# Two scatter-add targets, 59 tiles and a mask shift among the tiles, in a two-layer graph and expert kernel

## Chip, core and metric

The kernel runs on one core of a Trainium2 chip. Times are microseconds (us) of device time of that core, from one execution of the whole program; the median of a few executions is given, with the lowest and highest. The profiled execution is a further one, and its own time stands beside its span. Engines are called TensorE (PE; its weight loads PEld), VectorE (DVE), ScalarE (ACT), GpSimd (POOL) and SyncE (SP); "SPq" and "ACTq" in a row are DMA issues of those engines.

## The reference

There are 3327 nodes with 256 features each and a 3327 x 3327 adjacency. Two layers follow each other; each is an attention over the neighbours and then a mixture of 8 experts of which every node uses 2.

```
x = x + gelu(graph_attention_0(layernorm(x), adj))        # 1 head
x = x + experts_0(layernorm(x))                            # 8 experts, hidden 512, top 2
x = x + graph_attention_1(layernorm(x), adj)               # 4 heads, plus projection of x
x = x + experts_1(layernorm(x))                            # 8 experts, hidden 1024, top 2

experts(x): logits = x @ gate + b; top 2 of softmax -> weights w
            out[n] = sum over the 2 experts e of n: w[n,e] * (gelu(x[n] @ W1[e] + b1[e]) @ W2[e] + b2[e])
```

## The kernel before

The nodes are padded to 26 tiles of 128 rows (T = 26, NP = 3328). All matmuls of the experts are fp32. The program is a row of blocks; in a block every engine has its own stream, and a block ends when all engines have ended theirs. In order: the first attention, the first experts' routing, the first experts' tiles, a small block that reads x back, the second attention (a block for its values and reaches, a block for the attention itself), the second experts' routing and their tiles.

**Routing.** Each node has two slots, one for each of its experts. Slots of one expert are packed into tiles of 128 slots; `expert_of[g]` is the expert of tile g, `slot_row[:, g]` the DRAM row of each slot and `slot_w[:, g]` its weight. Slots that hold no node point at spare rows behind the 3328. The kernel before runs RUN_TILES = 2T + 8 = 60 tiles and keeps SLOT_TILES = 62 columns.

**A tile g** (slot s = g % 2 of every ring of two) goes through these steps, which each engine does in the order of g:

- SP (`tiles_sync`, L1594): when the hidden products of tile g are done, load W1 of tile g+2 into slot s (512 KB in the first experts, 1 MB in the second).
- POOL (`tiles_gpsimd`): L1611 gathers the 128 rows of tile g+4 from `xs` into one of four buffers `rx`; L1626 scatter-adds the weighted result `ry[s]` into the rows of `total` in DRAM (`xd` in the first experts, `out` in the second). The two slots of a node can lie in any two tiles, and an accumulating transfer reads, adds and writes, so the kernel lets only one scatter be in flight.
- PE (`tiles_tensor`): `hidden` of tile g+1 (L1637), the transposes `turn_x` of tile g+2 (L1644), the second product y of tile g (L1674), in this order.
- ACT (`tiles_scalar`): copies the transposed x (L1684, or L1688 in the second experts) and takes the Gelu of the hidden rows (L1703).
- DVE (`tiles_vector`): adds b2 (L1718) into `ysum`, multiplies by the slot's weight (L1721) into `ry[s]`.

The wait that orders the scatters, in POOL's stream:

```
pool.wait_ge(self.ry_ready[g % 2], g // 2 + 2)
if g > 0:
    pool.wait_ge(self.added, 16 * g)                 # scatter g-1 has landed
    pool.sem_inc(self.ry_free[(g - 1) % 2], 1)       # DVE may write ry of g+1
pool.indirect_dma_start(total[...], ... self.ry[g % 2], compute_op=ALU.add).then_inc(self.added, 16)
```

DVE waits on `ry_free[s]` before it adds b2 for the next tile of slot s. TensorE waits on `ry_ready[s]` before it writes the y bank of slot s again.

**Between the layers.** `xd` holds x plus the experts' sum. A block of its own reads it back into X with one DMA on SP (L1726, 3.4 MB), while DVE shifts the whole adjacency mask left by 3 bits as 32-bit words (L1904, 21632 words a partition, in place). Then semaphores are cleared, all engines meet, and the next block starts: bn_stats over the 26 tiles of X (L1735) for the layer norm, six loads of weights on SP (L340 to L350), and the values' products, for which TensorE waits for all six.

Of the kernel before, what the change touches and what calls it, by code (L numbers as in the profile page):

```python
# [28 lines left out]
ALU = mybir.AluOpType  # L29
# [24 lines left out]
RUN_TILES = 2 * T + 8  # L54
SLOT_TILES = RUN_TILES + 2
# [34 lines left out]
def program(nc, x_in, adjT, w0T, w0, r0, w1, w1T, uv1, proj_wT, bias1, proj_b1,  # L90
            gate0, gate_b0, m0w1, m0b1, m0w2, m0b2, gate1, gate_b1, ln_g1, ln_b1, m1w1, m1b1, m1w2, m1b2,
            qd, xd, xs, out):
    ctx = ExitStack()
    with ctx:
# [75 lines left out]
        spare_clean = sem("spare_clean")  # L170
        id_zero = sem("id_zero")
# [51 lines left out]
        class Attention:  # L223
            def __init__(self, L, tag):
# [54 lines left out]
                self.w_loaded = sem(tag + "w_loaded")  # L279
                self.stat = sem(tag + "stat")  # L280
# [54 lines left out]

            def values_sync(self, sp):
# [15 lines left out]
            def values_vector(self, v):  # L352
                L, H = self.L, self.L.H
                v.memset(self.ones_row[:, :], 1.0).then_inc(self.reach_best, 1)
                layer_norm_stats(v, self)
# [840 lines left out]
        class Experts:  # L1196
            def __init__(self, hidden, tag, weights_at, scratch_at, second_norm):
# [91 lines left out]
                def ring(n, size):  # L1289
# [33 lines left out]
                self.x_back = sem(tag + "x_back")  # L1323
# [10 lines left out]
                self.added = sem(tag + "added")  # L1334
                self.ry_free = [sem(f"{tag}ry_free{s}") for s in range(2)]
                start_at_one.extend(self.tp_ready + self.xt_ready + self.xn_ready + self.tx_ready + self.xgt_ready
                                    + self.h_ready + self.ht_ready + self.y_ready + self.ry_ready + self.ry_free
# [251 lines left out]
            def tiles_sync(self, sp, w1m, b1m, b2m):  # L1589
# [11 lines left out]
                with sp.Fori(0, RUN_TILES // 2) as i:  # L1601
                    for s in range(2):
                        sp.wait_ge(self.h_ready[s], i + 2)
                        load_w1(2 * i + s + 2, s)
                for s in range(2):
                    sp.wait_ge(self.w1_loaded[s], 16 * (RUN_TILES // 2 + 1))

            def tiles_gpsimd(self, pool, total):
# [7 lines left out]
                for g in range(RUN_TILES):  # L1616
                    if g + 4 < SLOT_TILES:
# [8 lines left out]
                    pool.indirect_dma_start(total[:, :],  # L1626
                                            bass.IndirectOffsetOnAxis(ap=slot_row[:, g:g + 1], axis=0),
                                            self.ry[g % 2], None, compute_op=ALU.add).then_inc(self.added, 16)
                pool.wait_ge(self.added, 16 * RUN_TILES)

            def tiles_tensor(self, pe):
# [24 lines left out]
                with pe.Fori(0, RUN_TILES // 4) as j:  # L1656
                    for q in range(4):
                        i, s = 2 * j + q // 2, q % 2
                        o = 1 - s
                        g = 4 * j + q  # L1660

                        pe.wait_ge(self.w1_loaded[o], 16 * (i + s + 1))
# [3 lines left out]

# [381 lines left out]
```

## Time and profile before

| | |
|---|---|
| median of 3 runs | 2111.42 us (2108.45 to 2119.23) |
| profiled execution, its own time | 2120.95 us |
| its span, first to last instruction | 2119.3 us |
| PE busy (share of span) | 1706.8 us (81%) |
| DVE, ACT, POOL busy | 973.2, 1045.1, 499.4 us (46%, 49%, 24%) |
| granted TensorE clock, mean | 0.916 |
| DMA moved | 188.84 MB, mean 89 GB/s |

Busy time is the time an engine spent in instructions; what is between is idle, and the profile names what ended each idle time. Over the span the first experts' tiles lie at 556 to 905 us, the block between the layers at 906 to 919, the second attention at 919 to about 1620 and the second experts' tiles at 1662 to the end. "Landing" of a DMA is the time from its issue on the engine to its last byte. A granted clock of 1.00 is TensorE at its full 2.4 GHz, 0.50 is 1.2 GHz.

### The profile page before, as it was taken

The page shows a single profiled execution, that of the slowest core. Times are in us where ns is not written, and L with a number is a line of the kernel's source. Part 1 is how long each engine was busy: PE and PEld are TensorE (multiplying, and loading weights), DVE is VectorE, ACT ScalarE, POOL GpSimd, SP SyncE. Part 2 cuts the span into 40 slices and gives each one's busy share as a digit, 9 for nine tenths or more (in the row PEclk, how much of TensorE's full clock was granted, in tenths as well). Part 3 has the DMA queues.
Part 4 walks back from the last instruction along what each step waited for, and adds up shares of the span by engine and source line. Part 5 has one row for each costly group of instructions (what it writes and reads, how often), then busy time and mean ns, then how long its engine had stood idle before and what let it go on. Part 6 is the DMA issues. An engine that isn't in the chain of part 4 may idle for free. (4 is left out here: it accounts for less than half of the span.)

```text
span 2119.3 us, 44107 instructions
## 1 busy us (share of the span) xinstructions
PE 1706.8 (81%) x13058; PEld 1560.1 (74%) x13059; DVE 973.2 (46%) x2091; ACT 1045.1 (49%) x2152; POOL 499.4 (24%) x565
## 2 busy tenths in 40 slices
PE   4659999955687778646489797897965799999998
PEld 3448888845676667535488797897965799999997
DVE  4548888875411111166576666765675311111111
ACT  1634444444144343302478787787854255445444
POOL 1100000000144444400750712600000133333332
PEclk9969999985799999968699999999985899999999
DMA  9930000023365565520000000000016466666665
GB/s 145 108 46 8 15 7 15 13 77 131 95 151 144 140 146 138 122 87 12 6 15 9 16 12 12 16 8 16 15 54 234 141 182 187 174 180 190 173 178 146
DMA packets 78483, 188.84 MB, mean 89 GB/s; under 512 B 9658, under 2 KB 49878, under 8 KB 69206
## 3 DMA queue, kind: packets, MB, share of 16 engines
q1 hardware_dynamic: 50630, 144.50, 20.7%
q0 software_dynamic: 26976, 43.07, 13.8%
q8 instruction: 29, 0.48, 0.1%
q10 hardware_dynamic: 816, 0.53, 0.1%
q14 instruction: 32, 0.26, 0.0%
HBM read 191.47 MB, written 29.83 MB: 104 GB/s over the span
## 5 line engine op out<-in xcount | busy, mean ns | idle before, releaser
L1185 PE MATMUL bank<-arena 128*128 128x195 bf16 x5408 | 478.6, 249 | 103.1 <-DVE arena L1086 44.4
L1185 PEld LDWEIGHTS bank<-arena 128*128 128x128 fp8e4 x5408 | 466.8, 98 | 114.8 <-issue 113.2
L996 ACT ACTIVATE arena<-arena,m_row 128x512 fp8e5<-128x512 f32 (+1 forms) x728 | 431.8, 677 | 131.1 <-DVE arena L1086 119.1
L1674 PE MATMUL bank<-arena,X 128*128 x1440 | 343.2, 389 | 29.4 <-issue 25.4
L1718 DVE TENSOR_TENSOR arena<-bank,X 128x256 f32<-128x256 f32 x120 | 50.9, 425 | 682.4 <-PE bank L1674 460.2
L1637 PEld LDWEIGHTS bank<-X,arena 128*128 128x128 f32 x2928 | 353.1, 195 | 6.8
L1637 PE MATMUL bank<-X,arena 128*128 128x128 f32 x2928 | 352.6, 278 | 0.0
L1674 PEld LDWEIGHTS bank<-arena,X 128*128 128x128 f32 x1440 | 268.1, 193 | 74.0 <-issue 41.6
L856 PE MATMUL bank<-arena 128*128 (+1 forms) x1352 | 299.6, 383 | 14.7 <-DVE arena L799 14.7
L856 PEld LDWEIGHTS bank<-arena 128*128 128x128 f32 x1352 | 257.0, 191 | 56.4 <-issue 20.6
L777 ACT ACTIVATE bank<-arena,s_all 128x384 f32<-128x384 f32 (+1 forms) x234 | 133.9, 573 | 183.0 <-DVE arena L791 175.8
L1084 DVE SCALAR_TENSOR_TENSOR arena<-arena 128x512 uint32<-128x512 uint32 (+2 forms) x196 | 131.9, 673 | 173.3 <-ACT arena L996 106.7
L1703 ACT ACTIVATE X<-bank,arena 128x128 f32<-128x128 f32 x720 | 199.3, 379 | 18.3 <-issue 17.6
L1611 POOL DMA_INDIRECT arena<-xs,slot_row x124 | 122.3, 986 | 203.3 <-POOLq L1847 164.7
L791 DVE SCALAR_TENSOR_TENSOR arena<-arena,d_all,bank 128x384 f32<-128x384 f32 (+1 forms) x234 | 139.7, 597 | 63.5 <-PE bank L856 47.2
L1688 ACT ACTIVATE X<-bank,arena 128x128 f32<-128x128 f32 x124 | 50.1, 454 | 237.9 <-PE bank L1644 237.9
L1626 POOL DMA_INDIRECT out<-X,slot_row x60 | 95.5, 1592 | 275.3 <-DVE X L1721 240.6
L1626 POOL DMA_INDIRECT xd<-X,slot_row x60 | 98.0, 1633 | 167.7 <-issue 140.6
L1585 POOL IOTA arena<- 128x128 f32 x2 | 0.5, 240 | 574.4 <-POOLq L1820 363.5
L1086 DVE SCALAR_TENSOR_TENSOR arena<-arena 128x512 uint32<-128x512 uint32 (+2 forms) x196 | 132.6, 677 | 0.0
L799 DVE TENSOR_TENSOR arena<-arena 128x384 f32<-128x384 f32 (+1 forms) x234 | 124.7, 536 | 0.0
L1684 ACT COPY X<-bank 128x256 f32<-128x256 f32 x62 | 23.1, 373 | 198.4 <-PE bank L1644 198.4
(204 smaller groups left out, 1406.0 us busy)
## 6 DMA issues: line engine op xcount, KB each, us to landing
arena<-m1w SPq DMA_DIRECT2D x70, 1024.0 KB, 5.8
arena<-m0w SPq DMA_DIRECT2D x70, 512.0 KB, 3.6
arena<-adjT POOLq DMA_DIRECT2D x26, 416.0 KB, 12.9
xs<-X SPq DMA_DIRECT2D x4, 1664.0 KB, 6.9
arena<-qd SPq DMA_DIRECT2D x25, 256.0 KB, 3.3
X<-x_in SPq DMA_DIRECT2D x2, 1664.0 KB, 11.5
xd<-X SPq DMA_DIRECT2D x13, 256.0 KB, 2.2
X<-xd SPq DMA_DIRECT2D x1, 3328.0 KB, 12.0
```

The source lines that it names most:

```text
L777: a.activation(self.exp_bank[s][:, 0:nt * P], self.rows[r][:, 0:nt * P], ACT.Exp, bias=s_all[:, at(c, 1)]).then_inc(self.exp_ready[s], 1)
L791: v.scalar_tensor_tensor(out=self.prob[q][:, 0:w], in0=self.rows[r][:, W:W + w], scalar=d_all[:, at(c, 1)], in1=self.exp_bank[s][:, 0:w], ...
L799: v.tensor_tensor(self.prob[q][:, 0:w], self.prob[q][:, 0:w], mask[:, at(c * NP + b * W, w)], ALU.min).then_inc(self.prob_ready[q], 1)
L856: last = pe.matmul(bank[3 * r + n][:, 0:D + 1], self.prob[q][:, n * P:(n + 1) * P], V[:, at(c * VW, D + 1)], start=False, stop=False, skip ...
L996: last = a.activation(self.sign[slot].bitcast(F8W)[:, q * W:q * W + nt * P], self.row[r][:, 0:nt * P], ACT.Sigmoid, scale=STEEP, bias=self ...
L1084: v.scalar_tensor_tensor(out=pos, in0=sg, scalar=1, in1=m, op0=ALU.logical_shift_left, op1=ALU.bitwise_and).then_inc(self.pos_ready, 1)
L1086: v.scalar_tensor_tensor(out=neg, in0=sg, scalar=0x08080808, in1=m, op0=ALU.bitwise_xor, op1=ALU.bitwise_and).then_inc(self.neg_ready[slot ...
L1185: last = pe.matmul(bank[r * NT + n][:, kind * KW:(kind + 1) * KW], self.split[slot][kind].bitcast(F8)[:, q * W + n * P:q * W + (n + 1) * P ...
L1626: pool.indirect_dma_start(total[:, :], bass.IndirectOffsetOnAxis(ap=slot_row[:, g:g + 1], axis=0), self.ry[g % 2], None, compute_op=ALU.ad ...
L1637: last = pe.matmul(bank[2 * s + c // 4][:, c % 4 * P:(c % 4 + 1) * P], self.W1[s][:, k * HID + c * P:k * HID + (c + 1) * P], self.rxt[s][: ...
L1674: last = pe.matmul(bank[5 + s][:, 0:D], self.ht[s][:, c * P:(c + 1) * P], self.W2[:, at(e * (HC * D) + c * D, D)], start=(c == 0), stop=(c ...
L1703: last = a.activation(self.ht[s][:, c * P:(c + 1) * P], bank[2 * s + c // 4][:, c % 4 * P:(c % 4 + 1) * P], ACT.Gelu, bias=self.b1[:, at(e ...
```

## The change

1. RUN_TILES and SLOT_TILES become 2T + 7 = 59 (`2 * T + E - 1`). The loops no longer run `hidden`, `turn_x` and W1 loads for tiles beyond the last; the last one to three tiles stand behind the loops as straight code (both experts).
2. First experts: even tiles scatter-add into `xd`, odd ones into a new DRAM tensor `xe`. POOL no longer waits for the scatter before; DVE waits for the scatter of tile g-2 (`added[s]`) before it writes `ysum` and `ry[s]`. The second experts still have one target and keep POOL's wait; there too DVE waits on `added[s]` directly, and `ry_free` is gone.
3. `xe` is filled with zeros by one DMA of POOL (27 x 128 rows of 1 KB) in the block of the first attention.
4. The block between the layers is gone. The mask shift is cut into 26 slices of 832 words, one ahead of each pair of tiles 2 to 53 in DVE's tile loop of the first experts.
5. The second attention's first block loads `xd` into X in four parts on SP and `xe` into the arena in four parts on ACT; for each part DVE adds the two and runs bn_stats on its tiles. The six loads of weights move from SP's queue to ACT's, behind the four parts.

```diff
-RUN_TILES = 2 * T + 8
-SLOT_TILES = RUN_TILES + 2
+RUN_TILES = 2 * T + E - 1
+SLOT_TILES = RUN_TILES
...
+            def back_load(self, eng, which):
+                tiles = [T * c // self.BACK for c in range(self.BACK + 1)]
+                to, of = ((X, xd), (words(V_AT, T * D), xe))[which]
+                for c in range(self.BACK):
+                    a, b = tiles[c], tiles[c + 1]
+                    eng.dma_start(to[:, a * D:b * D].rearrange("p (t d) -> p t d", d=D),
+                                  of[a * P:b * P, :].rearrange("(t p) d -> p t d", p=P)).then_inc(self.x_back[c], 16)
+            def back_vector(self, v):
...
+                    v.wait_ge(self.x_back[c], 32)
+                    v.tensor_tensor(X[:, a * D:b * D], X[:, a * D:b * D], other[:, a * D:b * D], ALU.add
+                                    ).then_inc(self.x_whole, 1)
+                    v.wait_ge(self.x_whole, c + 1)
+                    for t in range(a, b):
+                        v.bn_stats(stats[:, at(t * 6, 6)], X[:, at(t * D, D)]).then_inc(self.stat, 1)
...
-                    if g > 0:
-                        pool.wait_ge(self.added, 16 * g)
-                        pool.sem_inc(self.ry_free[(g - 1) % 2], 1)
-                    pool.indirect_dma_start(total[:, :],
+                    if n_to == 1 and g > 0:
+                        pool.wait_ge(self.added[(g - 1) % 2], 16 * ((g - 1) // 2 + 1))
+                    pool.indirect_dma_start(totals[g % n_to][:, :],
...
-                        v.wait_ge(self.ry_free[s], i + 1)
+                        v.wait_ge(self.added[s], 16 * i)
...
+                slices = 26
+                size = MASK_WORDS // slices
+                for s in range(2):
+                    tile(0, s)
+                with v.Fori(1, slices + 1) as i:
+                    if not self.second_norm:
+                        m32 = words(MASK_AT, MASK_WORDS).bitcast(U32)[:, at((i - 1) * size, size)]
+                        v.tensor_scalar(m32, m32, 3, None, ALU.logical_shift_left)
+                    for s in range(2):
+                        tile(i, s)
...
+                pool.dma_start(xe.rearrange("(t p) d -> p t d", p=P),
+                               zeros[:, :].bitcast(F32).rearrange("p (o d) -> p o d", o=1).to_broadcast([P, T + 1, D])
+                               ).then_inc(xe_clean, 16)
...
-        with nc.Block() as block:
-            @block.sync
-            def _(sp):
-                X0.back_sync(sp)
-            @block.vector
-            def _(v):
-                m32 = words(MASK_AT, MASK_WORDS).bitcast(U32)
-                v.tensor_scalar(m32, m32, 3, None, ALU.logical_shift_left)
...
             @block.sync
             def _(sp):
+                A1.back_load(sp, 0)
                 give_ones(sp, q1_ones)
-                A1.values_sync(sp)
                 A1.own_row_sync(sp)
...
             @block.scalar
             def _(a):
+                A1.back_load(a, 1)
+                A1.values_sync(a)
```

## Rows read from the trace of the kernel before

**Rows 1.** Busy time by stretch: bounds, length, PE, PEld, DVE, ACT, POOL with counts, clock, DMA share, GB/s

```profile
577.49:589.20 11.71, 11.70 (x80) 10.63 (x79) 2.38 (x6) 7.67 (x21) 5.92 (x5) 1.00 0.79 187
620.00:820.00 200.00, 153.02 (x945) 130.09 (x944) 28.61 (x74) 78.66 (x202) 96.13 (x73) 1.00 0.59 143
1700.00:2090.00 390.00, 390.00 (x2691) 367.70 (x2691) 41.87 (x108) 195.84 (x567) 139.08 (x108) 1.00 0.64 181
```

**Rows 2.** Waits, 620 to 880 us: who waited for whom, total, times, longest

```profile
DVE arena L1718 <- POOLq L1625: 192.8, 42, 6.1
...
PE bank L1644 <- DMA arena<-xs,slot_row: 34.9, 40, 2.4
```

**Rows 3.** Timeline, 700 to 722 us: start, length, engine, instruction, idle before it

```profile
702.91 1.71 POOL L1626 DMA_INDIRECT xd<-X,slot_row  x1 [2.59 <-issue]
...
704.92 0.99 POOL L1611 DMA_INDIRECT arena<-xs,slot_row  x1 [0.30 <-issue]
...
707.97 0.42 DVE L1718 TENSOR_TENSOR arena<-bank,X 128x256 f32<-128x256 f32 x1 [4.81 <-POOLq L1625]
...
708.20 0.44 PE L1644 MATMUL bank<-ident,arena 128*128 128x128 f32 x2 [0.96 <-DMA arena<-xs,slot_row]
...
708.56 1.59 POOL L1626 DMA_INDIRECT xd<-X,slot_row  x1 [2.65 <-issue]
```

**Rows 4.** Timeline, 574 to 590 us, the first tiles

```profile
574.67 0.35 DVE L1721 TENSOR_SCALAR X<-arena,slot_w 128x256 f32<-128x256 f32 x1
575.31 1.64 POOL L1626 DMA_INDIRECT xd<-X,slot_row  x1 [13.93 <-DVE X L1721]
...
575.98 1.89 PE L1674 MATMUL bank<-arena,X 128*128 x8
...
581.68 1.95 PE L1637 MATMUL bank<-X,arena 128*128 128x128 f32 x16
...
589.41 1.95 PE L1637 MATMUL bank<-X,arena 128*128 128x128 f32 x16
```

**Rows 5.** DMA queues, 575 to 903 us: packets, MB, share of 16 engines

```profile
q1 hardware_dynamic: 8352, 30.41, 30.2%
q0 software_dynamic: 11376, 15.34, 27.7%
```

**Rows 6.** DMA issues, 577 to 590 us: count, size, median us to landing

```profile
arena<-m0w SPq DMA_DIRECT2D x4, 512.0 KB, 4.2
```

**Rows 7.** Line L1626: ns minimum/median/maximum, and landing in 575 to 903 us

```profile
L1626 POOL DMA_INDIRECT xd<-X,slot_row x60: 1546/1588/1711, 575.3 to 899.2; - x60
...
DMA to landing us min/median/max: 3.7/4.6/5.9
```

**Rows 8.** Timeline, 880 to 985 us: last scatter, read-back block, statistics

```profile
899.16 1.55 POOL L1626 DMA_INDIRECT xd<-X,slot_row  x1 [2.97 <-DMA xd<-X,slot_row]
905.97 0.40 SPq L1726 DMA_DIRECT2D X<-xd  x1
906.00 11.43 DVE L1904 TENSOR_SCALAR arena<-arena 128x21632 uint32<-128x21632 uint32 x1 [11.05 <-PEq L1868]
...
919.50 8.59 DVE L1735 BATCH_NORM_STATS2 stats<-X  x26
...
928.12 0.20 DVE L1740 TENSOR_TENSOR mv<-stats 128x26 f32<-128x26 f32 x1
```

**Rows 9.** The page's DMA issues: count, size, median us to landing

```profile
X<-xd SPq DMA_DIRECT2D x1, 3328.0 KB, 12.0
```

**Rows 10.** Timeline, 2095 to 2120 us, the last tiles of the second experts

```profile
2099.85 3.62 PE L1674 MATMUL bank<-arena,X 128*128 x16
...
2107.10 3.62 PE L1674 MATMUL bank<-arena,X 128*128 x16
...
2112.62 1.55 POOL L1626 DMA_INDIRECT out<-X,slot_row  x1 [3.96 <-DVE X L1721]
```

**Rows 11.** Timeline, 520 to 600 us, one step of the first routing

```profile
531.72 0.99 DVE L1485 TENSOR_TENSOR X<-tile_no,arena 128x806 f32<-128x806 f32 x1
```

More of the change, by code:

```diff
@@ L91, in program @@
             gate0, gate_b0, m0w1, m0b1, m0w2, m0b2, gate1, gate_b1, ln_g1, ln_b1, m1w1, m1b1, m1w2, m1b2,
-            qd, xd, xs, out):
+            qd, xd, xe, xs, out):
     ctx = ExitStack()
@@ L279, in __init__ @@
                 self.w_loaded = sem(tag + "w_loaded")
+                self.x_back = [sem(f"{tag}x_back{c}") for c in range(4 * (H > 1))]
+                self.x_whole = sem(tag + "x_whole")
                 self.stat = sem(tag + "stat")
@@ L1655, in tiles_tensor, with tile @@
                 pe.wait_ge(self.w2_loaded, 16 * 8)
[L1656 to L1660, printed above, removed]
+                def tile(j, q):
+                    i, s = 2 * j + q // 2, q % 2
+                    o = 1 - s
+                    g = 4 * j + q
+                    left = 4 if not isinstance(j, int) else RUN_TILES - 1 - g
+                    if left >= 1:
                         pe.wait_ge(self.w1_loaded[o], 16 * (i + s + 1))
@@ L1725, in back_sync, with tile @@
[L1725 to L1735 removed]
+                def tile(i, s):
+                    g = 2 * i + s
+                    e = v.value_load(expert_of[0:1, at(g, 1)], min_val=0, max_val=E - 1)
+                    v.wait_ge(self.y_ready[s], i + 2)
+                    if not isinstance(i, int) or i > 0:
+                        v.wait_ge(self.added[s], 16 * i)
+                    v.tensor_tensor(self.ysum[s], bank[5 + s][:, 0:D], self.b2[:, at(e * D, D)], ALU.add
+                                    ).then_inc(self.ysum_ready, 1)
+                    v.wait_ge(self.ysum_ready, g + 1)
+                    v.tensor_scalar(self.ry[s], self.ysum[s], slot_w[:, at(g, 1)], None, ALU.mult
+                                    ).then_inc(self.ry_ready[s], 1)
@@ new lines, in tiles_vector @@
+                slices = 26
+                size = MASK_WORDS // slices
+                for s in range(2):
+                    tile(0, s)
[3 more added lines that the diff above has]
+                        v.tensor_scalar(m32, m32, 3, None, ALU.logical_shift_left)
+                    for s in range(2):
+                        tile(i, s)
+                with v.Fori(slices + 1, RUN_TILES // 2) as i:
+                    for s in range(2):
+                        tile(i, s)
@@ L1736, in layer_norm_stats @@
+                tile(RUN_TILES // 2, 0)
+        def layer_norm_stats(v, sems, nth=1, done=False):
+            if not done:
+                with v.Fori(0, 2) as half:
+                    for q in range(PAIRS):
+                        t = half * PAIRS + q
+                        v.bn_stats(stats[:, at(t * 6, 6)], X[:, at(t * D, D)]).then_inc(sems.stat, 1)
             v.wait_ge(sems.stat, T * nth)
```

112 lines of the change are left out of this document (59 added, 53 removed).

## The prediction

> **What bounds the kernel now.** I read the table of busy time by stretch first. In the first experts' tiles the engines leave room: over 620 to 820 us TensorE is busy 153 of 200 us at full clock, GpSimd 96, and the DMA engines 59% [rows 1]. So no engine is the bound, and the waits have to say what is. Over 620 to 880 us (48 tiles) VectorE waits 192.8 us for GpSimd's semaphore instruction at L1625, the one that follows the wait for the scatter before, and TensorE waits 34.9 us for gathers at L1644 [rows 2].
>
> The timeline shows the ring. A scatter starts at 702.91 and the next at 708.56, 5.65 us later; GpSimd works 1.71 us on the first, issues a gather for 0.99, then sits idle for 2.65 until the scatter has landed [rows 3]. VectorE starts its add at 707.97, when the semaphore is given. The gather of four tiles ahead stands behind the scatter in GpSimd's stream, so it comes late too, and TensorE's transpose at 708.20 has waited 0.96 for it [rows 3]. The period of a tile is the scatter's way through: 323.85 us between the first scatter (575.31) and the last (899.16) over 59 intervals [rows 4, 8], 5.49 us each.
>
> How fast could it be? The first tiles tell, before the backlog of scatters reached TensorE. There the hidden products of two tiles apart start at 581.68 and 589.41: 7.73 us, 3.87 a tile [rows 4]. In that stretch TensorE is busy for all of its 11.7 us, and the DMA share is 79% [rows 1]. The second experts are different: TensorE is busy for all 390 us from 1700 to 2090 [rows 1], and a tile takes 7.25 [rows 10]. They are bound by it.
>
> **The change part by part.** The sum is made against the profiled execution: span 2119.3 us, own time 2120.95, which is 9.5 above the median of 2111.42. I take the difference in us from the one to the other unchanged.
>
> *Two targets.* The wait for scatter g-1 goes. What is late next? Four candidates for the period of a tile:
> - TensorE: 3.87 us [rows 4].
> - GpSimd: scatter 1.59, gap 0.30, gather 0.99 [rows 3, 7], and 0.29 from the end of VectorE's multiplication (574.67 + 0.35) to the scatter [rows 4]: 3.17 us. If each scatter is as long as the longest, 1.71, 3.29.
> - The ring of one slot, now over two tiles: add and multiplication 0.9, start 0.3, landing 4.6 (longest 5.9) [rows 3, 4, 7], some 0.2 for the semaphore: 6.0 to 7.3 us for two tiles, so 3.0 to 3.65.
> - W1: a load can be issued when hidden g ends and is needed when hidden g+2 starts, 2 x 3.87 - 1.95 = 5.8 us later. In the free stretch loads landed in 4.2 us [rows 6], which leaves 1.6 for issue and queueing.
>
> All four are under 3.87 but the first, and none by much. The DMA engines give the reason for a little more: they were taken 57.9% of a 5.49 us period [rows 5], 3.18 us of work a tile, or 82% of 3.87. The free stretch ran at 79% without a wait of TensorE, though with fewer scatters. I take 3.95 us, near the row of the free stretch; the bounds are 3.8 (TensorE no slower than its best pair) and 4.4 (W1 landing 1.7 us later than it did, at 5.9, which sets (1.95 + 0.9 + 5.9) / 2; the 0.9 of issue lag is my estimate from the 1.6 that are free).
>
> The y product of tile 1 starts at 575.98 [rows 4] in both. Tile 58 follows 57 periods later; at 3.95 that is 801.1, less 1.0 because the last tile has no hidden product ahead of it and waits only for its Gelu (1.95 saved, some 1 for the wait, an estimate): 800.1. Product 2.0, VectorE and start 1.3, landing 3.9 (between the least and the median [rows 7], since no W1 load is beside it): 807.2. The last scatter of before landed at 899.16 + 3.9 = 903.1. Gain 95.9.
>
> *The shift.* 11.43 us in one instruction beside the 12.0 us load [rows 8, 9] cost nothing before, and 26 slices of 0.44 us cost nothing now, since VectorE is busy 28.6 of 200 us [rows 1]. At worst each slice delays VectorE's tile by 0.44, within the slot ring's slack. There is another way in which it can cost. GpSimd's scatter takes 1.71 instead of 1.59 when VectorE's 0.35 us multiplication runs at its start [rows 3, 7], so 0.12 is what an overlap cost here.
>
> The Trainium skill ("SBUF — State Buffer", Who interferes with whom) says more: a tensor_scalar in a 2-port mode and GpSimd lock each other out for the whole instruction. By that, 0.44 every second tile and the whole 0.35 each tile would be added to GpSimd's 3.17, an estimate of 3.74 a tile; the sum, which goes by TensorE's 3.87, would stay. The trace has the 0.12 only, and nowhere a slice beside a scatter.
>
> *Between the layers.* Before: from landing (903.1) to the layer norm's statistics (928.12) 25.0 us: 2.9 to the next block's DMA at 905.97, 13.5 of load and block change, 8.6 of bn_stats [rows 8]. After: the same 2.9, and 1.2 of the 1.5 that lie between the load's landing (905.97 + 12.0) and the first bn_stats, for clearing semaphores and the meeting of all engines; then 6.8 MB instead of 3.4. The load of before took 12.0 us for 3.4 MB [rows 9]; with 2.3 of it taken as start (an estimate) it ran at 350 GB/s. I take the two queues as sharing that rate, for one queue already feeds all 16 engines [rows 5]: 19.5 + 2.3 + 0.5 for issues = 22.3. Behind the last quarter come an add of 1792 columns, 1.9 (VectorE did 806 in 0.99, of which a part is fixed [rows 11]; 256 in 0.42 [rows 3]), and 7 bn_stats at 0.33, 2.3. Together 30.7: 5.7 lost. Bounds: if the queues add their rates, 12.0 + 0.5 + 4.2 + 4.1 = 20.8, a gain of 4.2; if they take turns at the full 24.0, a loss of 7.8. The six weight loads are queued behind `xe` on ScalarE's queue, and everything that TensorE does next waits for them; 1 MB more (by the tensors' shapes) is 3 us behind 22.3, landing about when the statistics are ready, so hidden. The sqrt on ScalarE stands behind ten issues of 0.40 [rows 8], 4 of the 26 us there are.
>
> *59 tiles and straight ends.* In the second experts y of tile 58 starts at 2099.85, of 59 at 2107.10, and takes 3.62; the other 3.6 of the period of 7.25 are the hidden products [rows 10]. Now y of tile 58 is the last and has none ahead of it: it ends 7.25 + 3.6 = 10.9 earlier. Its scatter may meet the one before still landing, so I give back 0.4: gain 10.5. Bounds: 7.3 (if a wait for Gelu takes the place of the hidden product) and 10.9.
>
> *Smaller tables.* Twelve operations of 806 columns at 0.99 [rows 11] become 767: 0.04 each, 0.5 a layer, with the matmuls 0.6; gain 1.2.
>
> *Zeroing `xe`.* 3.4 MB in the first attention, whose window has hundreds of us with DMA nearly idle; its first row loads could be 2 us late. Taken as 0.5, bounds 0 and 3.
>
> Sum: 95.9 - 5.7 + 10.5 + 1.2 - 0.5 = 101.4. The profiled execution's 2120.95 would be 2019.5, and the median 2111.4 - 101.4 = 2010. Each 0.1 us of period is 5.7 us.
>
> **Rivals.**
> - *Transfers become the bound.* With 82% of the DMA engines taken, W1 or the scatters land later and the period is 4.15 to 4.7. For it: landings grew from 3.7 to 5.9 already [rows 7], and 4.2 for W1 in the dense stretch. Against: no wait for W1 at 79% [rows 1]. At 4.4 the gain is 101.4 - 57 x 0.45 = 76: 2036.
> - *GpSimd becomes the bound.* 3.17 is the least; if the slices and VectorE's multiplications shut it out for their whole length and each start takes 0.9 rather than 0.3, it takes 3.17 + 0.22 + 0.35 + 0.6 = 4.34 a tile: 22 less, 2032. The rule quoted above is what would bring it about; the row's 0.12 speaks against.
> - *The order moves only a little.* Something else keeps the tile near 5.2, for instance gathers that still wait for their place in GpSimd's stream: gain 101.4 - 57 x 1.25 = 30, 2081. Against: with the scatter's wait gone GpSimd has 0.7 us to spare in each tile.
> - *Slower than before.* Two accumulating scatters in flight slow each other, so that the slot ring sets the period. It is (1.4 + landing) / 2; the gains are used up at 3.95 + 101.4 / 57 = 5.73 us, that is from a landing of 10.1 us, where the longest of 60 was 5.9 [rows 7]. At 11 the period is 6.2 and the time 2138.
>
> **How the numbers follow.** Forecast (period 3.8 to 4.15, so 2001 to 2021, and 1997 with part of the reload's bound) 0.65; transfers 0.15; GpSimd 0.08; little moved 0.08; slower 0.02; 0.02 for others near no change. The likeliest is 2010. The range of 8 in 10 takes in the transfers' and GpSimd's cases: 1997 to 2038. A change under 0.5% (10.6 us) is about what a measurement of this kernel can't tell from none; faster by more than that 0.95, within 0.03, slower 0.02.
>
> **What would show it.** Hidden products of the first experts 3.85 to 4.0 us apart, TensorE busy over 95% between 580 and 800 us at clock 1.00, VectorE's wait for POOLq gone and replaced by a wait for the y product; GpSimd waiting for VectorE ahead of each scatter. Rows of TensorE waiting for `arena<-m0w` would show the first rival; scatters above 1.8 us the second. The statistics would end some 30 us after the last scatter's landing, and the last scatter of the program would start 6.7 us before the end, as it does now. The forecast fails if the free stretch was free only because few scatters were in flight.

## The result, and the profile of the changed kernel

| | before | after |
|---|---|---|
| median | 2112.49 us (2108.45 to 2119.23, 4 runs) | 2016.78 us (2016.21 to 2018.66, 4 runs) |
| profiled execution, its own time | 2120.95 us | 2017.3 us |
| its span | 2119.3 us | 2015.4 us |
| PE busy (share of span) | 1706.8 us (81%) | 1665.5 us (83%) |

The ratio of the times is 0.9528, with a 95% interval of 0.9506 to 0.9551: the changed kernel is faster by 4.7%. The forecast was 2010, with a range of 1997 to 2038. Between the profiled executions 103.65 us are gained, between the medians 95.7.

The busy time by stretch, after (columns as in [rows 1]):

```profile
600.00:760.00 160.00, 159.81 (x1077) 146.29 (x1076) 44.45 (x104) 90.24 (x230) 112.08 (x84) 1.00 0.79 203
...
805.00:850.00 45.00, 16.51 (x67) 13.14 (x68) 27.25 (x70) 4.12 (x9) 0.00 (x0) 0.61 0.57 176
...
1640.00:2000.00 360.00, 360.00 (x2491) 339.58 (x2490) 38.90 (x100) 179.26 (x523) 126.13 (x97) 1.00 0.63 177
```

In the first experts' tiles TensorE is now busy 159.8 of 160 us, where it was 153 of 200 [rows 1]. The DMA share is 79%, the same as in the free stretch of before. The waits of that stage, 580 to 790 us:

```profile
DVE arena L1764 <- PE bank L1705: 137.0, 52, 3.2
...
POOL xd L1655 <- DVE X L1767: 26.1, 27, 1.3
POOL xe L1655 <- DVE X L1767: 22.7, 28, 1.9
...
DVE arena L1764 <- DMA xe<-X,slot_row: 5.8, 2, 3.0
PEld bank L1667 <- DMA arena<-m0w: 0.5, 1, 0.5
```

VectorE's wait for GpSimd's semaphore [rows 2] is gone; it waits for TensorE's y product (L1705). GpSimd waits for VectorE's result (L1767) ahead of each scatter (L1655). Only twice did VectorE wait for a scatter two tiles back, and once TensorE for a load of W1. The same in time, 701 to 708 us:

```profile
701.47 1.95 PE L1667 MATMUL bank<-X,arena 128*128 128x128 f32 x16
...
702.34 0.35 DVE L1767 TENSOR_SCALAR X<-arena,slot_w 128x256 f32<-128x256 f32 x1
702.76 0.59 DVE L1777 TENSOR_SCALAR arena<-arena  x1
702.97 1.84 POOL L1655 DMA_INDIRECT xe<-X,slot_row  x1 [0.75 <-DVE X L1767]
...
705.12 0.99 POOL L1641 DMA_INDIRECT arena<-xs,slot_row  x1 [0.30 <-issue]
...
705.45 1.95 PE L1667 MATMUL bank<-X,arena 128*128 128x128 f32 x16
...
707.05 1.59 POOL L1655 DMA_INDIRECT xd<-X,slot_row  x1 [0.94 <-DVE X L1767]
```

The scatters are 4.08 us apart here, and GpSimd is ready 0.75 and 0.94 us before their data are. Hidden products start at 701.47, 705.45 and, behind what is shown, 709.18: 7.71 us for two tiles. The scatters and the shift by their lines (lengths in ns, minimum/median/maximum):

```profile
L1655 POOL DMA_INDIRECT xd<-X,slot_row x30: 1547/1591/1632, 575.5 to 797.0; - x30
L1655 POOL DMA_INDIRECT xe<-X,slot_row x29: 1547/1841/1867, 579.2 to 795.2; - x29
...
L1777 DVE TENSOR_SCALAR arena<-arena x26: 587/594/595, 578.8 to 772.3; - x26
```

The DMA queues, 575 to 800 us:

```profile
q1 hardware_dynamic: 7920, 28.84, 45.4%
q0 software_dynamic: 11051, 14.79, 31.3%
```

The boundary between the layers, 797 to 834 us:

```profile
797.02 1.55 POOL L1655 DMA_INDIRECT xd<-X,slot_row  x1 [0.30 <-issue]
804.68 6.24 SPq L348 DMA_DIRECT2D X<-xd  x4
804.69 7.73 ACTq L348 DMA_DIRECT2D arena<-xe  x4
812.44 5.10 ACTq L368 DMA_DIRECT2D arena<-w  x1
...
823.42 0.45 ACTq L378 DMA_DIRECT2D arena<-proj_b  x1
...
827.16 2.02 DVE L358 TENSOR_TENSOR X<-X,arena 128x1792 f32<-128x1792 f32 x1 [0.66 <-DMA arena<-xe]
829.22 2.38 DVE L362 BATCH_NORM_STATS2 stats<-X 128x6 f32<-128x256 f32 x7
830.36 1.85 PE L447 MATMUL bank<-arena 128*128 128x8 f32 x8 [34.80 <-DMA arena<-proj_b]
...
831.66 0.18 DVE L1796 TENSOR_TENSOR mv<-stats 128x26 f32<-128x26 f32 x1
```

The last of the eight loads let VectorE go at 827.16, 22.5 us after the first was issued. And the end of the program, where [rows 10] showed it before:

```profile
1999.50 7.07 PE L1705 MATMUL bank<-arena,X 128*128 x32
...
2004.46 1.55 POOL L1655 DMA_INDIRECT out<-X,slot_row  x1 [5.38 <-DVE X L1767]
...
2008.89 1.55 POOL L1655 DMA_INDIRECT out<-X,slot_row  x1 [2.88 <-DMA out<-X,slot_row]
```

The y products of the last two tiles follow each other without a hidden product between them.

Stage by stage, the profiled execution before against that after (in us, bounds by the first and last scatters and the first `mv<-stats`, the start of the layer norm's statistics):

| | before | after | gain | forecast |
|---|---|---|---|---|
| start to first scatter | 575.31 | 575.48 | -0.2 | +0.1 (tables, zeroing) |
| first to last scatter, first experts | 323.85 | 221.54 | 102.3 | 95.9 |
| last scatter to statistics | 28.96 | 34.64 | -5.7 | -5.7 |
| statistics to first scatter, second experts | 756.58 | 759.97 | -3.4 | +0.6 (tables) |
| first to last scatter, second experts | 427.92 | 417.26 | 10.7 | 10.5 |
| last scatter to end | 6.68 | 6.51 | 0.2 | 0 |
| sum | | | 103.9 | 101.4 |

### The profile page after: what moved, and what is told of

Read it like the earlier page. It is cut to its first block and busy times, and to the rows that moved or that the text cites. A ratio compares the mean times of both kernels' runs of the same rounds, so it can differ in the third digit from the quotient of the medians.

```text
span 2015.4 us, 43515 instructions
## 1 busy us (share of the span) xinstructions
PE 1665.5 (83%) x12926; PEld 1536.0 (76%) x12927; DVE 980.1 (49%) x2116; ACT 1033.3 (51%) x2127; POOL 497.2 (25%) x558
## 5 line engine op out<-in xcount | busy, mean ns | idle before, releaser
L1667 PEld LDWEIGHTS bank<-X,arena 128*128 128x128 f32 x2832 | 337.8, 194 | 6.5 <-DMA arena<-m0w 0.5
L1667 PE MATMUL bank<-X,arena 128*128 128x128 f32 x2832 | 338.2, 277 | 0.1
L1705 PE MATMUL bank<-arena,X 128*128 x1416 | 329.2, 383 | 4.6 <-ACT X L1740 4.4
L884 PE MATMUL bank<-arena 128*128 (+1 forms) x1352 | 299.6, 383 | 15.5 <-DVE arena L827 15.5
L1705 PEld LDWEIGHTS bank<-arena,X 128*128 128x128 f32 x1416 | 260.8, 191 | 42.0 <-issue 11.0
L1740 ACT ACTIVATE X<-bank,arena 128x128 f32<-128x128 f32 x708 | 195.9, 379 | 25.4 <-issue 19.9
L1641 POOL DMA_INDIRECT arena<-xs,slot_row x118 | 116.6, 988 | 201.2 <-issue 117.5
L1725 ACT ACTIVATE X<-bank,arena 128x128 f32<-128x128 f32 x118 | 47.7, 454 | 223.7 <-PE bank L1674 223.7
L1655 POOL DMA_INDIRECT out<-X,slot_row x59 | 93.9, 1592 | 270.2 <-DVE X L1767 267.4
L1048 POOL TENSOR_TENSOR arena<-arena,neg_sj 128x130 f32 x46 | 27.2, 592 | 275.3 <-PEq L1221 143.9
```

The source lines that it names most:

```text
L884: last = pe.matmul(bank[3 * r + n][:, 0:D + 1], self.prob[q][:, n * P:(n + 1) * P], V[:, at(c * VW, D + 1)], start=False, stop=False, skip ...
L1641: pool.indirect_dma_start(self.rx[g % 4], None, xs[:, :], bass.IndirectOffsetOnAxis(ap=slot_row[:, g:g + 1], axis=0)).then_inc(self.rx_loa ...
L1667: last = pe.matmul(bank[2 * s + c // 4][:, c % 4 * P:(c % 4 + 1) * P], self.W1[s][:, k * HID + c * P:k * HID + (c + 1) * P], self.rxt[s][: ...
L1705: last = pe.matmul(bank[5 + s][:, 0:D], self.ht[s][:, c * P:(c + 1) * P], self.W2[:, at(e * (HC * D) + c * D, D)], start=(c == 0), stop=(c ...
L1740: last = a.activation(self.ht[s][:, c * P:(c + 1) * P], bank[2 * s + c // 4][:, c % 4 * P:(c % 4 + 1) * P], ACT.Gelu, bias=self.b1[:, at(e ...
```

## The experiments

Each kernel is the changed one with the edit shown, run beside the kernel before; ratios are to the kernel before. Kernels with a single execution have no interval.

**The second target taken back.** Even and odd tiles add into `xd` again, with GpSimd's wait; everything else of the change stays.

```diff
-        experts_blocks(X0, [xd, xe], a1_ones, gate0, ...
+        experts_blocks(X0, [xd], a1_ones, gate0, ...
```

> The changed kernel with one edit undone: in the first experts all tiles scatter-add into xd again, and GpSimd waits for the scatter before, as in the second experts. xe is still zeroed, loaded and added. Theory (the wait for the one scatter in flight set the period): the scatters of the first experts are 5.3 to 5.5 us apart again, VectorE or TensorE wait behind that ring, and the time is 2016.8 + 57 x 1.55 + some 4 us of tail = 2104 to 2112 us. Rival (the gain came mostly from fewer tiles, straight ends and the moved shift): the period stays under 4.5 us and the time under 2055 us.

Measured 2106.95 us, ratio 0.9946 (0.9919 to 0.9972). Eight of its nine executions lie between 2093.28 and 2109.83; the ninth took 3023.88, at a mean granted clock of 0.554 where the others had 0.912 to 0.918. What lowered it is not known, and without it the median would be 2106.43. The waits of 620 to 860 us:

```profile
DVE arena L1764 <- DMA xd<-X,slot_row: 185.9, 44, 5.2
...
POOL xd L1655 <- DMA xd<-X,slot_row: 107.7, 43, 3.4
```

The ring is back: 312.46 us from the first scatter to the last over 58 intervals, 5.39 each. The kernel before took 5.49 in one profile and 5.08 in another (below), so this lies between them. So it is the second target that brings the stage's gain, down to 3.82 an interval; of the shift, the straight ends and VectorE's direct wait on `added`, together, no part of it is seen.

**Only the shorter tiles.** One target, the old block between the layers, the shift in one piece, no `xe`; 59 tiles, straight ends and the smaller tables stay.

```diff
-        experts_blocks(X0, [xd, xe], a1_ones, gate0, ...
+        experts_blocks(X0, [xd], a1_ones, gate0, ...
+        with nc.Block() as block:      # sync: one load of xd into X; vector: the whole shift
...
-                A1.back_load(sp, 0)
+                A1.values_sync(sp)
```

> Only part 1 of the change: 59 tiles, smaller tables and straight ends in both experts, with one target, the read-back block with the whole mask shift, and no xe. Theory: 10.5 us from the end of the second experts, one tile of about 5.4 us in the first, 1.2 us from the tables, so 17 us under the kernel before: about 2095 us. The difference to the run with one target is the price of reading and adding two buffers, 5 to 6 us by the trace. Rival (straight code behind the loops costs instruction loading of several us at each end): 2100 us or more, with gaps of over 2 us at the ends of the loops.

Measured 2097.53 us (2087.84 to 2102.82), ratio 0.9912 (0.9877 to 0.9948). Its scatters are 5.34 us apart, and the statistics come 28.56 us after the last one, as before (28.96). It lies 9.4 us under the kernel above. Between the last scatter of the first experts and the first of the second there are 788.5 us here and 795.6 there, 5.6 of it up to the statistics: the new way of reading back costs something there too, and it has no use with one target.

**The kernel before, once more,** to see how much of its time varies and where.

> The kernel before once more, for a second profile. Its runs spread over 12 us, those of the changed kernel over 2.5 us, and the profiled execution of before lies 8.5 us above its median. Theory (the ring of scatters makes the time of the first experts' tiles depend on DMA landings and on stalls of TensorE that lower its clock): the stretch from the first to the last scatter differs from the 323.9 us of the first profile by several us, and the rest of the program by less than 2. Rival (the spread lies elsewhere, in the mask load or the attentions): the stretch is the same within 1 us.

Measured 2096.7 us. Its scatters:

```profile
L1626 POOL DMA_INDIRECT xd<-X,slot_row x60: 1547/1588/1708, 575.3 to 875.2; - x60
```

From first to last 299.84 us, 5.08 a tile, against 323.85 in the profiled execution of before. The spans differ by 24.2 us (2095.1 and 2119.3), this stage by 24.0; the rest takes 1795.2 and 1795.5. So these two executions of the kernel before differ in the ring of scatters and nowhere else. The landings make the difference: added up over the stage's 60 scatters they come to 275.8 us in the first profile (4.6 in the middle) and 251.9 here (3.9), and the rest of a period, from a landing to the next scatter, is 0.88 on average in both. Why they land sooner here is not known. This execution is also faster than all 17 others of the kernel before in its set (2104.34 to 2122.57). In eight executions of the changed kernel and its variants with two targets and whole tiles (the two of the changed kernel, and those with thirteen parts, three shifts, the shift taken out, no load of `xe` and the two early reloads) the stage took 221.4 to 222.7 us.

**The changed kernel, once more,** beside three of its variants.

> The changed kernel once more, on the chip of the next two runs, for a comparison without the spread of the kernel before. Both theories: 2016 to 2018 us, its runs within 3 us, and 221.5 us from the first to the last scatter of the first experts.

Measured 2019.32 us (2017.44 to 2020.13), ratio 0.9534 (0.951 to 0.9558). Scatters 222.0 us from first to last, then 34.40 to the statistics. The same program's median was 2016.78 in the first set of runs: 2.5 us are between two sets, and less than that is not told apart across sets. The two profiles differ by 2.8 us in their spans, and by 3.1 in the stretch from the statistics to the second experts' first scatter (759.97 and 763.06): what varies in the changed kernel lies there and not in the first experts' tiles.

**No load of `xe`.** The odd tiles' sums are left out of the second layer's input.

```diff
-                    v.wait_ge(self.x_back[c], 32)
-                    v.tensor_tensor(X[:, a * D:b * D], X[:, a * D:b * D], other[:, a * D:b * D], ALU.add ...
+                    v.wait_ge(self.x_back[c], 16)
...
-                A1.back_load(a, 1)
```

> The changed kernel without the load of xe and without the adds: the second layer works on xd alone, so the odd tiles' sums are left out. It prices the second buffer in the read-back. Theory (the two loads share one rate of some 350 GB/s, so the second costs its bytes): from the first load's issue to the layer norm's statistics 27.0 falls to 15.5 us, that is 12 us of load, 2.4 of bn_stats of the last quarter and 1; 11 us faster, about 2006 us. Rival (two queues add their rates): the loads of one buffer take as long as those of two, only the adds of 1.9 us go, 2015 us.

Measured 2010.62 us (2007.56 to 2011.92), ratio 0.9494 (0.9465 to 0.9523), 8.7 us under the changed kernel of the same set. The boundary:

```profile
805.21 5.16 SPq L348 DMA_DIRECT2D X<-xd  x4
805.21 0.48 ACTq L365 DMA_DIRECT2D arena<-w  x1
...
821.93 2.39 DVE L359 BATCH_NORM_STATS2 stats<-X 128x6 f32<-128x256 f32 x7 [0.42 <-DMA X<-xd]
...
824.37 0.18 DVE L1793 TENSOR_TENSOR mv<-stats 128x26 f32<-128x26 f32 x1
```

From issue to statistics 19.2 us, against 27.0 with both loads (804.68 to 831.66). I had worked out 15.5, with the 12.0 of a load alone [rows 9]. But half of `xd` now shared its rate with the weights on the other queue, and it landed 16.7 us after its issue. So the second load costs 7.8 us, and the second queue adds no rate that is seen: 3.4 MB on one took 12.0 us [rows 9], 6.8 MB on two 22.5.

**Thirteen parts instead of four** in the reload.

```diff
-            BACK = 4
+            BACK = 13
```

> The changed kernel with the read-back in 13 parts of two tiles each instead of 4 parts. Behind the last landing stand an add of 512 columns and 2 bn_stats, about 1.3 us, instead of 4.4 us. Theory (the last part's VectorE work is on the path): 2 to 3 us faster, 2014 to 2015 us. Rival (ScalarE's queue takes its issues more slowly than the loads move, the third and later parts of xe are late, and the weights land after the statistics): same or up to 5 us slower.

Measured 2014.01 us (2010.07 to 2016.1), ratio 0.9526 (0.95 to 0.9553). The boundary:

```profile
802.99 10.93 SPq L348 DMA_DIRECT2D X<-xd  x13
802.99 11.86 ACTq L348 DMA_DIRECT2D arena<-xe  x13
...
826.31 0.68 DVE L358 TENSOR_TENSOR X<-X,arena 128x512 f32<-128x512 f32 x1
827.02 0.75 DVE L362 BATCH_NORM_STATS2 stats<-X 128x6 f32<-128x256 f32 x2
```

The statistics come 32.45 us after the last scatter, 2.2 less than with four parts: the add and the bn_stats behind the last part fell from 4.4 to 1.4 us, and not all of it came out at the end, since VectorE now has 0.69 + 0.75 a part for 13 parts and runs nearly without a pause from the third on. The whole time's interval overlaps that of the changed kernel, and the medians, 2.8 us apart, are of two sets, so the 2.2 us are shown by the trace alone.

**The shift three times as long.** Three shifts by one bit in place of one by three.

```diff
-                        v.tensor_scalar(m32, m32, 3, None, ALU.logical_shift_left)
+                        for _n in range(3):
+                            v.tensor_scalar(m32, m32, 1, None, ALU.logical_shift_left).then_inc(self.shifted, 1)
+                            v.wait_ge(self.shifted, 3 * i - 2 + _n)
```

> The changed kernel with each slice of the mask shift done as three shifts by 1 instead of one by 3: three VectorE instructions of 0.59 us in the same mode and place, 1.8 us and their waits for each pair of tiles. Theory (VectorE and GpSimd have room in a pair of 7.7 us, and an overlap delays a scatter by some tenths of a us): the period stays 3.86 us and the time 2015 to 2019. Rival (the Trainium skill's rule, SBUF - State Buffer, Who interferes with whom: such an instruction and GpSimd lock each other out for its whole length, so 1.2 us more go onto GpSimd's 6.7 us of a pair, which makes 7.9 and more than TensorE's 7.7): scatters beside the slices take 2.5 us and more, the period is 3.95 to 4.2 and the time 2022 to 2036.

Measured 2017.07 us (2012.92 to 2017.95), ratio 0.9552 (0.9498 to 0.9606). One pair of tiles:

```profile
701.93 1.95 DVE L1779 TENSOR_SCALAR arena<-arena  x3
702.14 1.84 POOL L1656 DMA_INDIRECT xe<-X,slot_row  x1 [0.76 <-DVE X L1768]
```

The shifts of the whole stage by their line (ns, minimum/median/maximum):

```profile
L1779 DVE TENSOR_SCALAR arena<-arena x78: 585/594/704, 578.0 to 772.7; - x78
```

VectorE shifts from 701.93 to 703.88, and the scatter that starts at 702.14 takes 1.84 us, as beside one shift. The scatters' stage took 221.52 us (221.54 with one). These are three instructions of 0.59 us, though, and not one of three times the length. The scatter starts 0.21 us into the first, as it does with a single shift, and is lengthened by 0.25 where 0.38 of that shift was left. So the run shows that VectorE has room for 1.4 us more in a pair of tiles (1.95 for 0.59); it does not show what one long shift would do to a scatter.

The Trainium skill ("SBUF — State Buffer", Who interferes with whom) has the second of the two engines shut out until the first one's instruction is over, where VectorE's is a `tensor_scalar` in a 2-port mode. For the start of the scatter the trace agrees roughly (0.25 of the 0.38 left), for the rest of it not: the scatter is running when the second shift comes, 0.41 us after its start, and that shift takes its 0.59 us, while the third, at 1.04, takes 0.70.

**The shift out of the tiles,** in one piece at the start of the second layer.

```diff
-                    if not self.second_norm:
-                        m32 = words(MASK_AT, MASK_WORDS).bitcast(U32)[:, at((i - 1) * size, size)]
-                        v.tensor_scalar(m32, m32, 3, None, ALU.logical_shift_left)
...
+                v.tensor_scalar(m32, m32, 3, None, ALU.logical_shift_left)
                 A1.back_vector(v)
```

> The changed kernel with the mask shift taken out of the tile loop and done in one instruction of 11.4 us ahead of the adds of the read-back. Theory (the slices cost nothing among the tiles; here 8 us of the shift lie in the wait for the first quarter, and VectorE's chain of 11.4 + 17 us is 1 to 2 us longer than the 27 us of the reload): the tile stretch is the same within 0.5 us, the scatters into xe take 1.59 us instead of 1.84, and the time is 1 to 3 us above the changed kernel's, 2018 to 2020. Rival (the slices hold up the tiles): the stretch from the first to the last scatter is several us shorter than 221.5 us.

Measured 2018.66 us (2015.46 to 2021.44), ratio 0.9562 (0.9508 to 0.9617). The scatters into `xe` are short again:

```profile
L1655 POOL DMA_INDIRECT xe<-X,slot_row x29: 1547/1587/1592, 575.8 to 792.8; - x29
```

And yet the stage took 222.64 us, not less. GpSimd's 0.25 us were paid out of its idle time ahead of the scatters. At the boundary 35.41 us instead of 34.64: there the 11 us shift hides behind the reload, nearly all of it.

**What comes next if TensorE has less to do.** Half of the first experts' hidden product is left out.

```diff
                     for c in range(HC):
-                        for k in range(KC):
+                        kk = KC if self.second_norm else 1
+                        for k in range(kk):
```

> The changed kernel with half of the first experts' hidden product left out (only the first 128 of the 256 features are multiplied), so that TensorE needs about 0.9 us less a tile, 2.97 us. It shows which bound stands next. Theory (GpSimd, with scatter 1.59 to 1.84, gather 0.99 and gaps): 3.4 us a tile, GpSimd without idle time beyond 0.3 us gaps and VectorE or TensorE waiting for it; time about 2016.8 - 57 x 0.45 = 1991. Rival 1 (DMA engines and W1): TensorE waits for the loads of W1, 3.3 to 3.7 us a tile. Rival 2 (landing of the scatter two tiles before): VectorE waits for DMA, 3.0 to 3.5 us a tile.

Measured 2013.81 us, in one execution. The scatters took 214.5 us, 3.70 a tile, though TensorE had 0.98 us less a tile. The whole time fell by less than these 7 us, since the stretch from the statistics to the second experts took 763.6 here, near the upper end of its spread. The waits of 580 to 785 us:

```profile
DVE arena L1765 <- DMA xe<-X,slot_row: 29.2, 13, 2.9
...
DVE arena L1765 <- DMA xd<-X,slot_row: 23.3, 10, 2.7
...
PEld bank L1675 <- DMA arena<-xs,slot_row: 13.2, 17, 1.4
```

The next bound is not GpSimd. VectorE waited 23 times for the scatter two tiles back, and TensorE for gathers. Landings took 5.1 and 5.3 us in the middle here, 6.1 at most, where one scatter in flight had 4.6 [rows 7].

**The same with an eighth of W1's bytes** from the third tile on (the hidden products then use old weights).

```diff
-                    sp.dma_start(self.W1[s], w1m[:, at(e * size, size)]).then_inc(self.w1_loaded[s], 16)
+                    part = size if (self.second_norm or isinstance(g, int) and g < 2) else size // 8
+                    sp.dma_start(self.W1[s][:, 0:part], w1m[:, at(e * size, part)]).then_inc(self.w1_loaded[s], 16)
```

> As the run with half of the first experts' hidden product left out, and from tile 2 on each load of W1 brings one eighth of its bytes, the rest of W1 staying that of the first two tiles. It takes most of the load off the DMA engines. If GpSimd is the next bound, the period stays at that of the run with full loads, within 0.05 us. If W1 or the DMA engines are, it falls to 3.2 us or lower.

Measured 1991.43 us, in one execution. 195.2 us of scatters, 3.37 a tile. The queues, 575 to 769 us:

```profile
q0 software_dynamic: 10812, 14.57, 46.8%
q1 hardware_dynamic: 7920, 3.61, 6.4%
```

With the hardware queue at a seventh, only one wait of VectorE for a scatter is left (1.7 us). Gathers landed in 2.8 us in the middle, where they took 3.8 with W1 loaded whole. So it was the W1 loads beside them that kept the transfers long enough to be waited for; the scatters' own landings are not in this profile. At 3.37 the period comes near GpSimd's 3.17 to 3.29, which the prediction had added up. GpSimd is still not the bound alone: ahead of the scatters into `xd` it waited 28 times for VectorE, 21.9 us in all. What sets the 3.37 stays open.

**The reload issued at the end of the tiles' block,** by SP and ScalarE themselves, in 13 parts, as soon as both `added` semaphores are complete.

```diff
+        def early_back(X_, eng, which):
+            for s in range(2):
+                eng.wait_ge(X_.added[s], 16 * (RUN_TILES // 2 + 1 - s))
+            A1.back_load(eng, which)
...
                     X_.tiles_sync(sp, w1m, b1m, b2m)
+                    if ln is None:
+                        early_back(X_, sp, 0)
```

> The changed kernel with the read-back in 13 parts and issued inside the block of the first experts' tiles, by SP and ScalarE as soon as the last scatters of both buffers have landed, so that the end of the block, the clearing of semaphores and the meeting of all engines run beside the loads. Theory: 2 us from the 13 parts and 3 to 4 us from the earlier issue, 2010 to 2012 us. Rival (issues of 13 parts on ScalarE hold up the block's end, or the engines meet later than the loads land): no more than the 2 us of the parts, 2014 to 2015 us.

Measured 2016.31 us (2015.41 to 2019.45), ratio 0.953 (0.9505 to 0.9554). The boundary:

```profile
794.55 1.55 POOL L1655 DMA_INDIRECT xd<-X,slot_row  x1 [0.31 <-issue]
798.41 10.56 ACTq L348 DMA_DIRECT2D arena<-xe  x13
...
810.89 0.69 DVE L358 TENSOR_TENSOR X<-X,arena 128x512 f32<-128x512 f32 x1 [16.76 <-PEq L1968]
```

The loads are issued 3.9 us after the last scatter instead of 7.7. But the block cannot end before ScalarE and SP have got rid of their 13 issues, 10.6 us, and VectorE's adds stand behind the block's end. The statistics come 34.43 us after the last scatter (34.40 in the changed kernel of the same set): nothing gained at that place. The median is 3.0 us lower and the executions overlap, so no gain of time is shown either.

**The same with the adds and the weights' loads in the tiles' block too.**

```diff
                     X_.tiles_vector(v)
+                    if ln is None:
+                        A1.back_vector(v)
...
+                        early_back(X_, a, 1)
+                        A1.values_sync(a)
```

> As the run with 13 parts issued inside the block of the first experts' tiles, and VectorE's adds and bn_stats and ScalarE's loads of weights stand in that block too, so that nothing of the read-back waits for the change of blocks. Theory (in the run before it the block's end held VectorE back for 10 us of issues): the loads start 4 us after the last scatter instead of 7.6, VectorE follows each part as it lands, and the statistics are ready some 30 us after the last scatter instead of 34.6: 4 us under the changed kernel, about 2013 to 2015 us. Rival (the change of blocks, now behind the reload, costs what it saved): 2016 to 2018 us.

Measured 2014.51 us (2012.35 to 2015.24), ratio 0.9528 (0.9501 to 0.9556). The boundary:

```profile
797.59 1.55 POOL L1655 DMA_INDIRECT xd<-X,slot_row  x1 [0.30 <-issue]
...
805.64 0.69 DVE L358 TENSOR_TENSOR X<-X,arena 128x512 f32<-128x512 f32 x1 [8.44 <-DMA X<-xd]
...
826.90 1.85 PE L447 MATMUL bank<-arena 128*128 128x8 f32 x8 [30.80 <-DMA arena<-proj_b]
...
828.86 0.17 DVE L387 COPY arena<-bank 128x16 f32<-128x16 f32 x1 [0.28 <-PE bank L447]
```

Statistics 29.3 us after the last scatter, 5.3 less; the copy behind the weights' product (L387) 31.3 after it instead of 36.4, since now that product comes last. Its executions lie all under those of the changed kernel run again (2017.44 to 2020.13), by 4.8 us in the medians. The two were not run in one set, and the changed kernel's medians have differed by 2.5 between sets; so the 5 us at the boundary are shown by the trace, and their full size in the time is not shown. Nor is this version shown to be faster than the one with thirteen parts alone, whose median is 2014.01 and whose ratio is 0.9526.

## Why the prediction was right, point by point

- **The bound.** Right. The scatters' ring was the bound and TensorE took its place: 99.9% busy, with the period of its free stretch. 56 periods of y products, from 576.05 to 791.94, give 3.855 us a tile. I had read 3.87 there [rows 4] and taken 3.95, for fear of the DMA load. The DMA engines' load came somewhat below what I had worked out (3.18 us a tile, 82% of the period): 76.7% over the stage with its ends, 2.92 us a tile, and 79% in the middle. It delayed TensorE once. The term was mis-sized by 0.095 x 56 = 5.3 us; another 1.1 lies in the last tile, whose y product followed at once and not 1 us later. That makes the 6.4 us between 95.9 and 102.3. (Two of my sums are 0.1 off in their last digit: the last landing's terms give 807.3 and not 807.2, those between the layers 30.6 and not 30.7.)
- **The four candidates.** Their order was wrong below the first, and it did not matter. I had put the slot ring at 3.0 to 3.65 a tile, GpSimd at 3.17. With TensorE's work cut the tile took 3.70, with waits for scatters' landings and gathers, and only without most of W1's bytes 3.37.
- **The rivals.** Transfers as the bound: not at this load, though it is what stands next, 0.15 us a tile behind TensorE. GpSimd: no; neither taking the shift out nor doing it as three instructions moved the stage (222.64 and 221.52 against 221.54). The order moving only a little: no gather was late. Slower: landings were 6.9 us at most where the profile gives them, far from the 10.1 from which it would have decided.
- **The shift.** Hidden, as said, but the price of a slice was 0.59 us, not 0.44, and it lengthened every second scatter by 0.25, not 0.12. VectorE and GpSimd both had room. I had also read the rows too simply: the second scatter of [rows 3], at 708.56, starts with the multiplication of 708.52 under way as well, and takes 1.59. What differs is that the multiplication of the lengthened one had started 0.11 us before it, and this one 0.04. So it isn't the overlap as such that costs.
- **Between the layers.** -5.7 as forecast, and its steps as well: 22.5 us for the two loads (22.3 forecast), the last add 2.02 (1.9), seven bn_stats 2.38 (2.3). The two queues came out as sharing one rate. One step was wrong without an effect: ten issues on ScalarE were taken as 4 us and took 19.2 (804.69 to 823.87), since the issues behind the loads' own took up to 5.10 us each. ScalarE had nothing else to do, and the weights' product ended at 832.2, some 1.2 us before its result was wanted. That margin was smaller than the text made it seem.
- **59 tiles.** +10.7 with 10.5 forecast.
- **Not foreseen: -3.4 us between the statistics and the second experts.** The two profiles of the kernel before have 756.58 and 756.01. Of the twelve profiles with 59 tiles eleven have 760.0 to 763.6, among them the changed kernel's two, 759.97 and 763.06, and one has 756.3 (with three shifts). So the kernels with 59 tiles are mostly slower here, but one of them is not, and one and the same program moves by 3.1; how much of the 3.4 belongs to the change is not settled. The old reload with 59 tiles has 759.98, so the reload and `xe` are not needed for it. By the order of VectorE's instructions the two main profiles part in the second attention, up to 4.6 us by 282 us after the statistics, and come back to 3.6 by its end; from there, through the routing, the new one gains 0.2, where I had 0.6 for the smaller tables. What moves the attention was not tried and stays open.
- **From the profiled execution to the median.** Here the forecast lost most. The sum was right to 2.2 us against the profiled execution: 2019.5 forecast, 2017.3 measured. Part of that is luck: 6.4 us too little for the tiles and 4.0 too much for the stretch behind the statistics stand against each other. Then I moved it down by the 9.5 us by which that execution lay above its median, and got 2010, 6.8 too low. The kernel before, run again, shows why this was most likely wrong: its two profiles differ only in the ring of scatters, so those 9.5 us were, as far as two profiles can tell, in the very stage that the change replaced, and went with it. No execution at the median was profiled. From the median I ought to have taken 101.4 less 9.5, which gives 2019.5 again.

## What to carry to other kernels

When a change removes a wait whose length varies, take the forecast from the profiled execution's own stages and let the stage after stand on its own terms; its excess over the median goes away with the wait. Profile the kernel before a second time, to see which stage varies. When two transfers that read, add and write must not overlap, a second target breaks the chain, and its price is to fill it with zeros and one more read of the whole target, here 5.7 us between the layers. A stretch of the kernel in which the bound has not yet set in (here the first three tiles) was the best row for what the period would be: 3.87 read there, 3.855 measured.

## What the hardware showed that was not expected

- GpSimd's scatter and a VectorE operation on one tensor (the multiplication, the shift) hold each other up or not by when each starts. A scatter that starts 0.10 to 0.12 us after the multiplication takes 1.66 to 1.71 us and not 1.59; one that starts 0.21 us into a shift takes 1.84. When it starts 0.04 to 0.08 us after the multiplication, the scatter takes its 1.59 and the multiplication 0.36 to 0.40 in place of 0.35. A multiplication that starts 0.52 to 0.82 us into a scatter ends 1.19 us after the scatter's start, and so takes up to 0.67 us. At nearly all other points both take their usual time. These are from the four profiles with one target; none of it moved the stage of the changed kernel.
- An issue of a DMA on ScalarE's queue takes 0.40 to 0.5 us when few are ahead of it. Behind 3.4 MB it took up to 5.10 us for one, and it holds the engine, and with it the end of the block.
- Two scatters in flight landed later (5.7 us in the middle and 6.9 at most in the changed kernel run again) than one (4.6 [rows 7], and 3.9 in the second profile of before), with W1 loads beside them in both. With two in flight VectorE waited for a landing only two or three times in the stage; with one the landings were all of the difference between two executions.
- The share of queue 0 in the transfers fell from 27.7% of 5.49 us [rows 5], 1.52 us a tile, to 31.3% of some 3.81, 1.19 us a tile, with about the same bytes. It is not the second target alone: with two targets, half the hidden product and an eighth of W1's bytes it is 46.8% of 3.29, 1.54 us. Nothing here explains it.
